# Layer-norm roots moved to GpSimd, min before exp replaced by Relu and exp on ScalarE, in a one-core transformer block

## The chip, the core and the metric

The kernel runs on one NeuronCore of a Trainium2 chip. The core has five engines with instruction streams of their own: TensorE (PE) for matrix products and transposes, VectorE (DVE), ScalarE (ACT), GpSimd (POOL) and SyncE (SP, which here only issues DMAs). They meet through semaphores. The metric is the device time of one execution in microseconds. One launch computes everything, in fp32.

## The reference

16 images of 3x96x96 pixels pass through one block of a vision transformer of width 192, with 38 tokens per image, so 608 tokens.

```python
h = patches @ W_emb + b_emb                  # 36 patches of 768 values, two class tokens in front
h = h + pos_embedding
xh = (h - mean(h)) / sqrt(var(h) + 1e-5)     # first layer norm
q, k, v = split(xh @ qkv_w.T)                # 12 heads of 16
f = lambda x: elu(x) + 1                     # feature map of queries and keys
# three linear attentions on f(q), f(k), v: a window of 12, every third key, 12 anchors;
# blended with softmax weights, then out_w
h = h + blended @ out_w.T
x2 = (h - mean(h)) / sqrt(var(h) + 1e-5)     # second layer norm
# 8 experts 192 -> 768 -> 192 with Relu, each token goes to its best 2,
# weighted by the two renormalised softmax probabilities
h = h + mixture(x2)
```

The feature map is elu(x) + 1 = max(x, 0) + exp(min(x, 0)).

## The kernel before

The tokens are cut into six groups: five of three images (114 tokens) and a last one of one image (38 tokens). A group lies with one token per partition, so the statistics of a layer norm are one column per group.

**Stages.** First the image patches are transposed and embedded (to about 26 us of the profiled execution). Then comes the attention as a software pipeline written out by hand, a loop over `t` on each of PE, DVE and ACT. In step `t` they project group `t`, take the key sums of group `t-1`, spread the queries of `t-2`, multiply keys and values of `t-3`, form the heads and the residual of `t-4` and start the router of `t-5` (to about 162 us). Each row is then scattered twice by indirect DMA to the region of its expert in HBM. At last a loop runs over 17 tiles of 128 slots (PE lines 940 to 976), and their results are added to the output sums by indirect DMA.

**What sets the order.** There is no planner. Each engine runs its instructions in the order of its block in the source, and a `wait_ge` holds all that stands behind it on that engine.

**A layer norm of a group.** DVE's `moments` (lines 1051 to 1054) writes mean and variance to `mv`. ACT's `root` (lines 1383 to 1387) takes the square root of the variance plus `epsv` into `rstd`. DVE's `normalise` (lines 1056 to 1061) waits for it, inverts it (line 1059) and makes the normalised tile (line 1060): `xhat` for the first layer, `tokens_out` for the second. PE transposes the tile of the first layer (`xhat_turn`, line 654), ACT copies it out (`xhat_out`), and PE projects queries and keys (line 677) and values (line 681). Only after the first of these does PE embed groups 2 and 3.

**The feature map.** In `features` (lines 1082 to 1097) DVE takes the minimum with zero of the 384 columns of queries and keys from PSUM into `qkmin`. ACT's line 1514 makes the exponential `qkexp`. DVE then combines them with the maximum into `qtok` and `ktok` (lines 1095, 1096).

**Function tables.** ACT's exponential and its square root are in different tables, and before an activation whose table is not loaded the program has an ACT_TABLE_LOAD. Copies and Relus are used with either.

**POOL.** After some small constants it waits for the bias of the experts (`b1_in`, line 1597) and splits it into a high and a low part (lines 1598, 1599). Then, group by group, it masks the values (line 1626, tile `vm`), spreads them over the heads (line 1635, tile `vexp`), copies normalised rows (`copy_row`) and issues the scatters (`scatter`, line 1612). The helper `link` puts a wait for an instruction's own completion behind each.

## Time and profile before

| | |
|---|---|
| median of 3 runs | 267.15 us |
| the runs | 267.15, 264.56, 270.74 us |
| profiled execution | 268.69 us, its span 266.9 us |
| mean granted PE clock | 0.855 of full speed |
| PE busy | 223.2 us (84%) |
| PE weight loads busy | 191.6 us (72%) |
| DVE busy | 150.5 us (56%), 464 instructions |
| ACT busy | 110.5 us (41%), 252 instructions |
| POOL busy | 73.7 us (28%), 103 instructions |

The span runs from the first to the last instruction of the profiled execution; what lies around it is 268.69 - 266.9 = 1.8 us. Busy time says how much an engine does, not whether somebody waits for it; for that the chain of waits is read, which is followed back from the last instruction. ScalarE's table loads count as busy. In the windows, "clock" is the TensorE clock that was granted, 1.00 being 2.4 GHz and 0.50 being 1.2 GHz.

### The profile page before, as it was taken

The page shows a single profiled execution, that of the slowest core. Times are in us where ns is not written, and L with a number is a line of the kernel's source. Part 1 is how long each engine was busy: PE and PEld are TensorE (multiplying, and loading weights), DVE is VectorE, ACT ScalarE, POOL GpSimd, SP SyncE. Part 2 cuts the span into 40 slices and gives each one's busy share as a digit, 9 for nine tenths or more (in the row PEclk, how much of TensorE's full clock was granted, in tenths as well). Part 3 has the DMA queues.
Part 4 walks back from the last instruction along what each step waited for, and adds up shares of the span by engine and source line. Part 5 has one row for each costly group of instructions (what it writes and reads, how often), then busy time and mean ns, then how long its engine had stood idle before and what let it go on. Part 6 is the DMA issues. An engine that isn't in the chain of part 4 may idle for free.

```text
span 266.9 us, 4475 instructions
## 1 busy us (share of the span) xinstructions
PE 223.2 (84%) x1340; PEld 191.6 (72%) x1340; DVE 150.5 (56%) x464; ACT 110.5 (41%) x252; POOL 73.7 (28%) x103
## 2 busy tenths in 40 slices
PE   6379699796999999998989955189999999999950
PEld 6268399564697967876767752079999999999940
DVE  5234318859476957858575688756768443433300
ACT  2343463767133453726242478035433342424210
POOL 4001260073305050414221335001324242423330
PEclk9658659799799999999985555559999999999995
DMA  7999999999400000000101298351333334341213
GB/s 121 132 233 172 235 287 271 266 225 289 123 10 0 0 4 1 2 0 0 29 2 26 56 324 205 80 136 42 70 47 59 47 54 52 52 55 18 29 15 85
DMA packets 26259, 25.73 MB, mean 96 GB/s; under 512 B 4970, under 2 KB 23261, under 8 KB 26221
## 3 DMA queue, kind: packets, MB, share of 16 engines
q1 hardware_dynamic: 22333, 22.16, 35.1%
q0 software_dynamic: 3568, 2.64, 7.8%
q10 hardware_dynamic: 336, 0.66, 1.7%
q8 instruction: 12, 0.20, 0.3%
q14 instruction: 10, 0.08, 0.1%
HBM read 16.56 MB, written 7.77 MB: 91 GB/s over the span
## 4 chain that ended last, share of the span: by engine, by line
PE 62%; DVE 14%; DMA 11%; issue 4%; ACT 3%; POOL 2%; SPq 2%; DVEq 0%; POOLq 0%; ACTq 0%
PE ps L950 11%; PE ps L973 10%; PE ps L580 5%; PE ps L708 4%; DMA wemb<-in_L_tok_W_emb 4%; DMA sums<-ys,xs 4%; PE ps L798 4%; PE ps L712 4%; PE ps L784 4%; PE ps L677 3%; PE ps L962 3%; PE ps L691 2%; DMA sent<-row,index 2%; SPq L428 1%; POOL sent L1612 1%
## 5 line engine op out<-in xcount | busy, mean ns | idle before, releaser
L1648 POOL DMA_INDIRECT sums<-ys,xs x17 | 26.3, 1546 | 67.0 <-ACT ys L1548 60.7
L973 PE MATMUL ps<-w2s,hidT 128*128 x204 | 36.1, 327 | 1.1 <-DVE hidT L1352 0.8
L973 PEld LDWEIGHTS ps<-w2s,hidT 128*128 128x128 f32 x204 | 33.2, 189 | 2.0 <-issue 1.6
L950 PE MATMUL ps<-w1hi,xhi 128*128 x68 | 25.3, 372 | 1.4 <-DVE xhi L1332 0.8
L1548 ACT ACTIVATE ys<-ps,xs 128x192 f32<-128x192 f32 x17 | 7.2, 421 | 40.0 <-PE ps L973 37.6
L1331 DVE TENSOR_TENSOR xlo<-ps,xhi 128x128 fp32r<-128x128 f32 x17 | 5.0, 292 | 29.8 <-ACT xend L1541 29.8
L784 PE MATMUL ps<-vm,ktok 114*96 114x288 f32 (+1 forms) x48 | 15.6, 406 | 5.0 <-DVE kvb L1147 5.0
L1635 POOL COPY vexp<-vtok 114x32 f32<-114x32 f32 (+1 forms) x36 | 8.0, 222 | 41.4 <-PE ps L712 39.5
L1430 ACT ACTIVATE qlb<-ps,cst 96x228 f32<-96x228 f32 (+1 forms) x36 | 12.1, 425 | 17.2 <-PE ps L746 17.2
L1612 POOL DMA_INDIRECT sent<-row,index x12 | 13.5, 1128 | 18.1 <-DVE row L1219 14.8
L708 PE MATMUL ps<-at,vexp 114*96 114x114 f32 (+1 forms) x144 | 18.2, 281 | 0.0
L798 PE MATMUL ps<-qlb,kT 96*114 96x342 f32 (+1 forms) x48 | 17.3, 442 | 0.5 <-DVE h L1068 0.5
L580 PE MATMUL ps<-wemb,xT 128*114 128x192 f32 (+1 forms) x72 | 17.3, 400 | 0.4 <-DMA wemb<-in_L_tok_W_emb 0.4
L708 PEld LDWEIGHTS ps<-at,vexp 114*96 114x96 f32 (+1 forms) x144 | 16.4, 181 | 1.2 <-issue 0.8
L1147 DVE TENSOR_TENSOR kvb<-ps,cst 96x288 f32<-96x288 f32 (+1 forms) x24 | 10.0, 418 | 11.5 <-PE ps L784 11.4
L1626 POOL TENSOR_TENSOR vm<-vtok,cst 114x576 f32<-114x576 f32 (+1 forms) x12 | 13.8, 1147 | 7.4 <-PE ps L784 5.8
L580 PEld LDWEIGHTS ps<-wemb,xT 128*114 128x114 f32 (+1 forms) x72 | 14.1, 214 | 1.9 <-DMA wemb<-in_L_tok_W_emb 0.7
L712 PE MATMUL ps<-qx,kvb 96*96 96x114 f32 (+1 forms) x128 | 15.3, 268 | 0.0
L950 PEld LDWEIGHTS ps<-w1hi,xhi 128*128 128x128 f32 x68 | 13.4, 196 | 2.4 <-issue 2.4
L962 PE MATMUL ps<-cst,hid 128*128 128x128 f32 x102 | 14.2, 276 | 0.0
L712 PEld LDWEIGHTS ps<-qx,kvb 96*96 96x96 f32 x128 | 13.8, 169 | 0.3 <-issue 0.3
L1346 DVE TENSOR_SCALAR hid<-ps 128x384 f32<-128x384 f32 x17 | 9.4, 554 | 7.6 <-PE ps L950 7.6
(197 smaller groups left out, 486.3 us busy)
## 6 DMA issues: line engine op xcount, KB each, us to landing
w2s<-in_L_ffn_W SPq DMA_DIRECT2D x8, 576.0 KB, 8.0
sent<-blank SPq DMA_DIRECT2D x1, 3977.0 KB, 32.3
w1s<-in_L_ffn_W SPq DMA_DIRECT2D x4, 768.0 KB, 17.1
xs<-sent SPq DMA_DIRECT2D x17, 96.0 KB, 1.9
w1s<-in_L_ffn_W SPq DMA_DIRECT2D x4, 384.0 KB, 18.5
w1hi<-w1hi SPq DMA_DIRECT2D x8, 192.0 KB, 3.9
ximg<-in_x SPq DMA_DIRECT2D x12, 96.0 KB, 9.3
w1s<-in_L_ffn_b SPq DMA_DIRECT2D x1, 792.0 KB
```

The source lines that it names most:

```text
L580: ins = pe.matmul(ps[6 + g % 2][0:n, 0:D], xT[:, k, t0:t0 + n], wemb[:, k, :], start=(k == 0), stop=(k == KCH - 1))
L708: pe.matmul(o, vexp[0:n, g % 2, i * HH + hh, :], at[0:n, g % 2, i * HH + hh, 0:w], start=(hh == 0), stop=False, skip_group_check=True)
L712: last = pe.matmul(o, kvb[:, g % 2, i, kind * PER + b, :], qx[:, g % 2, kind, i, b * GTOK:b * GTOK + w], start=False, stop=(kind == 1 and ...
L784: pe.matmul(ps[5][0:HALF, 0:imgs * HALF], ktok[0:n, g % KS, i * HALF:(i + 1) * HALF], vm[0:n, g % 2, i, kind * PER:kind * PER + imgs, :], ...
L798: pe.matmul(ps[6][0:n, 0:3 * n], kT[:, g % 3, i, 0:n], qlb[:, g % 2, i, 3 * (m % 2):3 * (m % 2) + 3, 0:n], start=True, stop=True).then_inc ...
L950: last = pe.matmul(ps[2 + c][:, 0:PASS], xx, of_expert(ww, expert), start=(n == 0), stop=(n == len(products) - 1))
L962: last = pe.transpose(ps[4 + c][:, k * 128:(k + 1) * 128], hid[:, (3 * c + k) * 128:(3 * c + k + 1) * 128], ident)
L973: last = pe.matmul(ps[6 + j % 2][:, 0:D], hidT[:, k, :], of_expert(w2s[:, :, k, :], expert), start=(k == 0), stop=(k == FCH - 1))
L1430: ins = ac.activation(qlb[:, g % 2, :, hh, 0:n], turned_q, ACT.Copy, scale=blk[:, hh * HD:hh * HD + 1])
L1612: po.indirect_dma_start(sent.rearrange("r p c -> (r p) c"), bass.IndirectOffsetOnAxis(ap=index[0:n, g, k:k + 1], axis=0), row[0:n, g, k, : ...
L1626: link(po.tensor_tensor(vm[0:n, g % 2, i], v.unsqueeze(1).broadcast_to([n, 2 * PER, HALF]), vmask[0:n, :].unsqueeze(2).broadcast_to([n, 2 ...
L1648: po.indirect_dma_start(sums, bass.IndirectOffsetOnAxis(ap=xs[:, j % NS, D + TAIL + 1:].bitcast(U32), axis=0), ys[:, j % 2, :], None, comp ...
```

## The change

The root and its inversion become one power: POOL adds the epsilon to the variance and raises the sum to -0.5, with two instructions on one column, each behind a semaphore wait. DVE's inversion goes. The minimum moves from DVE to ACT, as Relu of -x, and the exponential is taken of the negated result. With no square root left, ACT needs one table. POOL's programme is written out anew: the roots of groups 0 and 1 come right behind the bias split, those of groups 2 to 5 before the spread of the values, and those of the second layer after the `head_values` of two groups later; `copy_row` and `scatter` move around them.

```diff
--- before.py
+++ after.py
@@ -166,7 +166,7 @@
         stats = sb("stats", [GTOK, GROUPS, 6])
         mv = sb("mv", [GTOK, GROUPS, 2])
         rstd = sb("rstd", [GTOK, GROUPS])
-        epsv = sb("epsv", [GTOK, 1])
+        mhalf = sb("mhalf", [GTOK, 1])
         ones = sb("ones", [GTOK, 128])
         lead = sb("lead", [1, 1])
         row = sb("row", [GTOK, GROUPS, TOP, ROW])
@@ -335,7 +335,7 @@
 
         dv = sem("dv")
         dv_qx_zero = sem("dv_qx_zero")
-        dv_eps = sem("dv_eps")
+        dv_mhalf = sem("dv_mhalf")
         dv_posb_zero = sem("dv_posb_zero")
         dv_class_zero = sem("dv_class_zero")
         dv_one = sem("dv_one")
@@ -346,7 +346,6 @@
         dv_embedded = sem("dv_embedded")
         dv_moments = sem("dv_moments")
         dv_xhat = sem("dv_xhat")
-        dv_min = sem("dv_min")
         dv_features = sem("dv_features")
         dv_key_sums = sem("dv_key_sums")
         dv_image_sums = sem("dv_image_sums")
@@ -375,7 +374,7 @@
         ac_band_exp = sem("ac_band_exp")
         ac_anchor_exp = sem("ac_anchor_exp")
         ac_base = sem("ac_base")
-        ac_root = sem("ac_root")
+        ac_min = sem("ac_min")
         ac_weights = sem("ac_weights")
         ac_anchor_sum = sem("ac_anchor_sum")
         ac_xhat_turned = sem("ac_xhat_turned")
@@ -407,6 +406,7 @@
         gp_masked_values = sem("gp_masked_values")
         gp_head_values = sem("gp_head_values")
         gp_row = sem("gp_row")
+        gp_root = sem("gp_root")
 
         block = ctx.enter_context(nc.Block())
 
@@ -1019,7 +1019,7 @@
             ve.memset(ones[:], 1.0).then_inc(dv_one, 1)
             ve.memset(posb[0:1, :], 0.0).then_inc(dv_posb_zero, 1)
             ve.memset(xT[:].rearrange("p k (b s) -> p k b s", s=SEQ)[:, :, :, 0:2], 0.0).then_inc(dv_class_zero, 1)
-            ve.memset(epsv[:], EPS_LN).then_inc(dv_eps, 1)
+            ve.memset(mhalf[:], -0.5).then_inc(dv_mhalf, 1)
             ve.memset(qx[:], 0.0).then_inc(dv_qx_zero, 1)
             ve.wait_ge(dv_class_zero, 1)
 
@@ -1055,8 +1055,7 @@
 
             def normalise(g, n, src, dst, layer):
 
-                ve.wait_ge(ac_root, GROUPS * layer + g + 1)
-                link(ve.reciprocal(rstd[0:n, g:g + 1], rstd[0:n, g:g + 1]))
+                ve.wait_ge(gp_root, 2 * (GROUPS * layer + g + 1))
                 return ve.tensor_scalar(dst, src, mv[0:n, g, 0:1], rstd[0:n, g:g + 1],
                                         ALU.subtract, ALU.mult)
 
@@ -1083,10 +1082,6 @@
 
                 t0, n, _ = group(g)
                 src = ps[2][0:n, 0:2 * D]
-                ve.wait_ge(pe_qk, g + 1)
-                if g >= 1:
-                    ve.wait_ge(ac_exp, g)
-                ve.tensor_scalar(qkmin[0:n, :], src, 0.0, None, ALU.min).then_inc(dv_min, 1)
                 ve.wait_ge(ac_exp, g + 1)
                 if g >= 2:
                     ve.wait_ge(dv_queries, g - 1)
@@ -1378,13 +1373,6 @@
             ac.activation(anc[2][:], anc[1][:], ACT.Exp).then_inc(ac_anchor_exp, 1)
             ac.wait_ge(pe_base, 1)
             ac.activation(hbase[:], ps[5][0:GTOK, 0:D], ACT.Copy).then_inc(ac_base, 1)
-            ac.wait_ge(dv_eps, 1)
-
-            def root(g, layer):
-
-                t0, n, _ = group(g)
-                ac.wait_ge(dv_moments, GROUPS * layer + g + 1)
-                ac.activation(rstd[0:n, g:g + 1], mv[0:n, g, 1:2], ACT.Sqrt, bias=epsv[0:n, :]).then_inc(ac_root, 1)
 
             def xhat_out(g):
 
@@ -1394,8 +1382,6 @@
                               xhat_bank(g)[0:HALF, 0:2 * GTOK].rearrange("p (i t) -> p i t", i=2)[:, :, 0:n],
                               ACT.Copy).then_inc(ac_xhat_turned, 1)
 
-            root(0, 0)
-            root(1, 0)
             for m in range(4):
                 i, r3 = m // 2, m % 2
                 ac.wait_ge(pe_weights_turned, m + 1)
@@ -1491,7 +1477,6 @@
                     attention_over(ac)
                     ac.wait_ge(w1_in, 16 * E)
                     weights_high(0)
-                    root(GROUPS - 1, 1)
                     x2_out(GROUPS - 1)
                     weight(GROUPS - 2)
                     combine_out(0)
@@ -1508,10 +1493,12 @@
                     weight(t - 6)
                 if t < GROUPS:
                     t0, n, _ = group(t)
-                    ac.wait_ge(dv_min, t + 1)
+                    ac.wait_ge(pe_qk, t + 1)
+                    ac.activation(qkmin[0:n, :], ps[2][0:n, 0:2 * D], ACT.Relu, scale=-1.0).then_inc(ac_min, 1)
+                    ac.wait_ge(ac_min, t + 1)
                     if t >= 1:
                         ac.wait_ge(dv_features, t)
-                    ac.activation(qkexp[0:n, :], qkmin[0:n, :], ACT.Exp).then_inc(ac_exp, 1)
+                    ac.activation(qkexp[0:n, :], qkmin[0:n, :], ACT.Exp, scale=-1.0).then_inc(ac_exp, 1)
                     ac.wait_ge(pe_v, t + 1)
                     if t >= 3:
                         ac.wait_ge(gp_head_values, HH * (t - 2))
@@ -1519,12 +1506,7 @@
                 if t == 0:
                     anchors_out()
                     xhat_out(1)
-                    root(2, 0)
                     turning_over(ac)
-                if t + 3 < GROUPS:
-                    root(t + 3, 0)
-                if 0 <= t - 4 < GROUPS - 1:
-                    root(t - 4, 1)
                 if t >= GROUPS + 3:
                     weights_high(t - GROUPS - 2)
             weight(GROUPS - 1)
@@ -1613,11 +1595,16 @@
                                           bass.IndirectOffsetOnAxis(ap=index[0:n, g, k:k + 1], axis=0),
                                           row[0:n, g, k, :], None).then_inc(sent_in, 16)
 
-            patches_over(po)
-            for g in range(GROUPS):
+            def root(g, layer):
+
+                n = group(g)[1]
+                po.wait_ge(dv_moments, GROUPS * layer + g + 1)
+                link(po.tensor_scalar(rstd[0:n, g:g + 1], mv[0:n, g, 1:2], EPS_LN, None, ALU.add), gp_root)
+                link(po.tensor_tensor(rstd[0:n, g:g + 1], rstd[0:n, g:g + 1], mhalf[0:n, :], ALU.pow), gp_root)
+
+            def masked_values(g):
+
                 t0, n, imgs = group(g)
-                if g >= 4:
-                    copy_row(g - 4)
                 po.wait_ge(ac_v, g + 1)
                 if g >= 2:
                     po.wait_ge(pe_keys_values, 4 * (g - 1))
@@ -1625,21 +1612,50 @@
                     v = vtok[0:n, g % 3, i * HALF:(i + 1) * HALF]
                     link(po.tensor_tensor(vm[0:n, g % 2, i], v.unsqueeze(1).broadcast_to([n, 2 * PER, HALF]),
                                           vmask[0:n, :].unsqueeze(2).broadcast_to([n, 2 * PER, HALF]), ALU.mult), gp_masked_values)
-                if g == 0:
-                    turning_over(po)
-                    embedding_over(po)
-                    link(po.memset(vexp[:], 0.0), gp_vexp_zero)
+
+            def head_values(g):
+
+                n = group(g)[1]
                 if g >= 2:
                     po.wait_ge(pe_heads, g - 1)
                 for hh in range(HH):
                     link(po.tensor_copy(
                         vexp[0:n, g % 2].rearrange("p (i a) c -> p i a c", i=2)[:, :, hh, hh * HD:(hh + 1) * HD],
                         vtok[0:n, g % 3].rearrange("p (i c) -> p i c", i=2)[:, :, hh * HD:(hh + 1) * HD]), gp_head_values)
+
+            po.wait_ge(dv_mhalf, 1)
+            root(0, 0)
+            root(1, 0)
+            patches_over(po)
+            masked_values(0)
+            root(2, 0)
+            root(3, 0)
+            masked_values(1)
+            root(4, 0)
+            root(5, 0)
+            turning_over(po)
+            embedding_over(po)
+            link(po.memset(vexp[:], 0.0), gp_vexp_zero)
+            head_values(0)
+            head_values(1)
+            for g in range(2, GROUPS):
+                masked_values(g)
+                head_values(g)
+                root(g - 2, 1)
+                if g >= 3:
+                    copy_row(g - 3)
             po.wait_ge(sent_blank, 16)
-            for g in range(GROUPS - 4, GROUPS + 2):
-                if g < GROUPS:
-                    copy_row(g)
-                scatter(g - 2)
+            scatter(0)
+            copy_row(3)
+            scatter(1)
+            root(4, 1)
+            copy_row(4)
+            scatter(2)
+            root(5, 1)
+            copy_row(5)
+            scatter(3)
+            scatter(4)
+            scatter(5)
             po.wait_ge(sums_in, 16 * (GROUPS + 1))
             for j in range(TILES):
                 po.wait_ge(ac_answers, j + 1)
```

## Rows read from the trace of the kernel before

**Rows 1.** The chain that ended last, 27 to 47 us: start, us, what.

```profile
27.19 1.28 ACT L1387
...
28.49 0.48 ACT rstd L1387 x2
...
30.60 2.87 PE ps L677 x4
...
46.63 0.47 DVE qkmin L1089
```

**Rows 2.** Timeline of DVE: start, us, line, operation, what ended the idle time.

```profile
26.93 0.18 DVE L1054 BATCH_NORM_AGGREGATE mv<-stats 114x2 f32<-114x6 f32 x1
...
28.81 0.16 DVE L1059 RECIPROCAL rstd<-rstd 114x1 f32<-114x1 f32 x1 [0.85 <-ACT rstd L1387]
29.01 0.38 DVE L1060 TENSOR_SCALAR xn<-h,mv,rstd 114x192 f32<-114x192 f32 x1
```

**Rows 3.** Timeline of POOL, 27 to 36 us, columns as in rows 2.

```profile
27.30 0.19 POOL L1593 CAST blank<-cst 128x1 uint32<-128x1 f32 x1
...
32.73 0.81 POOL L1598 CAST b1hi<-b1s 8x768 fp32r<-8x768 f32 x1 [4.64 <-DMA w1s<-in_L_ffn_b]
33.62 1.80 POOL L1599 TENSOR_TENSOR b1lo<-b1s,b1hi 8x768 fp32r<-8x768 f32 x1
```

**Rows 4.** Timeline of PE.

```profile
29.45 0.61 PE L654 MATMUL ps<-cst,xn 114*96 114x114 f32 x2 [2.02 <-DVE xn L1060]
...
44.95 1.46 PE L677 MATMUL ps<-wT,xhT 96*114 96x384 f32 x4
...
129.47 0.41 PE L784 MATMUL ps<-vm,ktok 38*96 38x96 f32 x2
```

**Rows 5.** Windows: length, busy us (instructions) of PE, PEld, DVE, ACT, POOL; clock; DMA.

```profile
27.00:30.00 3.00, 0.97 (x8) 0.45 (x5) 1.89 (x8) 2.80 (x7) 0.85 (x5) 0.87 1.02 196
...
30.00:33.00 3.00, 2.46 (x5) 1.40 (x5) 0.00 (x0) 0.45 (x2) 0.27 (x1) 0.50 1.05 290
...
38.00:40.00 2.00, 2.00 (x9) 1.98 (x8) 0.00 (x0) 0.62 (x1) 0.84 (x1) 0.63 0.99 321
...
200.00:262.00 62.00, 57.08 (x369) 55.74 (x367) 23.86 (x51) 20.57 (x59) 21.48 (x14) 0.99 0.31 42
```

**Rows 6.** Groups of ACT by shape: count, busy us, mean ns, idle before.

```profile
L1387 ACT ACT_TABLE_LOAD x10 | 12.8, 1283 | 1.2 <-DVE mv L1054 1.1
...
L1514 ACT ACT_TABLE_LOAD x5 | 6.4, 1283 | 3.9 <-DVE qkmin L1089 3.8
...
L1445 ACT ACT_TABLE_LOAD x5 | 6.4, 1283 | 0.1
...
L1558 ACT ACTIVATE hid<-ps 128x384 f32<-128x384 f32 x17 | 8.4, 491 | 10.6 <-PE ps L950 10.6
...
L1514 ACT ACTIVATE qkexp<-qkmin 114x384 f32<-114x384 f32 x5 | 2.6, 523 | 11.7 <-DVE qkmin L1089 11.7
```

**Rows 7.** Group of DVE, columns as in rows 6.

```profile
L1089 DVE TENSOR_SCALAR qkmin<-ps 114x384 f32<-114x384 f32 (+1 forms) x6 | 3.3, 554 | 8.8 <-PE ps L677 8.8
```

**Rows 8.** The chain that ended last, 143 to 155 us.

```profile
143.56 0.19 DVE mv L1054
...
143.78 0.30 ACT rstd L1387
...
144.31 0.38 DVE row L1060
...
153.53 0.18 DVE mv L1054
```

**Rows 9.** Timeline of POOL, 112 to 152 us.

```profile
112.21 2.36 POOL L1626 TENSOR_TENSOR vm<-vtok,cst 38x576 f32<-38x576 f32 x2 [0.34 <-PE ps L784]
...
150.94 1.11 POOL L1612 DMA_INDIRECT sent<-row,index  x1 [0.30 <-issue]
```

**Rows 10.** Timeline of DVE, second layer norm of the third group.

```profile
114.89 0.18 DVE L1054 BATCH_NORM_AGGREGATE mv<-stats 114x2 f32<-114x6 f32 x1
```

## The prediction

> **What bounds the kernel now.** I read the 40 slices of the page first. TensorE (PE) is nearly full from the middle of the attention on, and in the last third, the mixture of experts, it is busy for 57.1 of 62 us at the granted clock 0.99 [rows 5]. The change touches nothing there, so it can only move the start of that stage. Then the chain of waits over the first 60 us. Up to 30.6 us it runs through the embedding, the moments of group 0, a table load, the root and the turned weights into the first projection of queries and keys [rows 1]. From there it is PE or VectorE (DVE) work that follows the projection of each group in a fixed order. The question is therefore when the first normalised tile is ready, and after that which removed or added piece stands on the chain.
>
> **The early stretch: the first root.** The moments of group 0 are ready at 26.93 + 0.18 = 27.11 us [rows 2]. ScalarE (ACT) then loads a table for 1.28 us and takes roots 0 and 1 from 28.49 [rows 1]. DVE inverts (28.81) and normalises from 29.01 [rows 2], and PE, which has nothing else it may do, turns that tile at 29.45 after 2.02 us of waiting [rows 4].
>
> The change puts this root on GpSimd (POOL), whose instructions run in the order written. Ahead of it stand the bias split (lines 1597 to 1599) and its wait for the bias DMA; the diff leaves both where they are. POOL waits 4.64 us for that DMA, makes the high part at 32.73, and the low part from 33.62 for 1.80 us, so it is free at 35.42 [rows 3]. The moments are done 8.3 us earlier and no longer decide. A root now costs two POOL instructions on one column, each followed by a wait on its own semaphore. A cast of one column takes 0.19 us on POOL, and the step over such a wait is 33.62 - (32.73 + 0.81) = 0.08 [rows 3]. I take the 0.19 for the addition. The power is in no row: it can cost what the cast does, 0.19, or, as software that computes more per element, up to the 1.80 us of the longest two-operand instruction here [rows 3]. I take 0.4, near the lower end, because it is one element per partition like the cast, where the 1.80 is for 768.
>
> So the first normalisation starts at 35.42 + 0.08 + 0.19 + 0.08 + 0.40 + 0.04 = 36.21 instead of 29.01: **+7.2 us** (0.04 is the step to another engine, 143.78 - 143.74 in [rows 8]). Behind the waiting POOL instruction queue the masks of the values, which need values that are themselves late by the same amount. Behind DVE's wait for the root stands the whole DVE programme, behind PE's wait the first projection. Nobody has independent work to fill the gap: PE stands idle from 27.43 to about 36.6. The table load of 1.28 us and the inversion leave this place, but they were finished long before POOL gets there, so they give nothing back here. No other early wait ends on something fixed in time, so I see nothing that absorbs the shift.
>
> **The other roots.** Before, from the end of the moments to the start of the normalisation took 144.31 - 143.74 = 0.57 us with the table already loaded [rows 8]. Now it is 0.04 + 0.19 + 0.08 + 0.40 + 0.04 = 0.75 us, 0.18 more. DVE waits for it at three places: group 2 in the first layer and the last two groups in the second (153.53 is the other one [rows 8]). Together **+0.5 us**. The bounds of the power make it -0.1 to +4.7.
>
> The other eight roots have slack, though POOL now waits for moments before it masks further values. The tightest is the third group of the second layer: its moments end at 115.07 [rows 10], so the masks of the last group, which started at 112.21 and took 2.4 us [rows 9], start at about 116 relative to this stretch; PE wants them at 129.47 [rows 4]. The root of the last group stands behind two scatters, of which the second ends at 152.05, before its moments at 153.70; for the group before it the same order has more slack [rows 8, 9]. Their cost is 0 with 1.6 us of cover; if that cover is gone, the excess counts in full.
>
> **The minimum and the exponential.** DVE loses 6 instructions of 0.55 us [rows 7] and ACT gains 6. The nearest row for the new Relu is the one on a 384-column PSUM tile, 491 ns, against 523 for the exponential from SBUF [rows 6]. The pair still follows the projection. On the chain it stands twice, for groups 1 and 2. For group 1 PE was done at 46.41 [rows 4] and DVE, busy with the query scaling, began the minimum at 46.56, on the chain from 46.63 [rows 1]; ACT is free and can begin 0.1 us sooner. For each of the two the piece itself is 0.55 against 0.49 [rows 6, 7]. For the later groups PE has other work and the pair is hidden. Together **-0.2 us**.
>
> **Inversions and table loads.** Twelve inversions of 0.16 us leave DVE [rows 2]. Those on the chain that the sums above do not hold are of groups 3, 4 and 5 in the first layer: **-0.5 us**. The 20 table loads, 10 + 5 + 5 of 1283 ns, free 25.7 us of ACT [rows 6]. ACT is not what is waited for: only one of the loads, at 27.19, is on the chain, and it is the one overtaken by the bias split. All others were issued while their operand was not there yet or beside PE work. They count 0, down to -1 us if one of them hid a wait that the trace gives to another engine. The single 59 ns memset is exchanged for another.
>
> **Sum.** 7.2 + 0.5 - 0.2 - 0.5 = **+7.0 us**. Against the profiled execution (span 266.9, time 268.69) that is 273.9 and 275.7. The median of the runs shown is 267.15, 1.5 below that execution, so I predict 267.15 + 7.0 = 274.15, in round numbers **274 us**. A measurement of this kernel tells about 2%, 5.3 us, from no change (its own runs spread from 264.56 to 270.74).
>
> **Rivals.**
> *A slow power.* If the power, or its first call, takes the 1.80 us of the far row, it counts at four places: 4 x 1.4 = 5.6 more, 279.8 us. Against: the first cast took 0.19 without a first-call cost [rows 3]. The Trainium skill (GPSIMD Engine Reference, section 2.1, Instruction dispatch) says that the first call to a freshly loaded GpSimd routine pays roughly 6 us; by that the sum would be 280, and the casts and multiplications here show no such pause. Chance 0.11.
>
> *Not slower, through PE's clock.* The granted clock falls from 1.0 to 0.50, its 1.2 GHz level, between 27 and 30 us and comes back at about 39.5 [rows 5], so some 9 us of work after the first wait run at half speed. If the clock returned at the same moment although work starts at 37.6, 7 us of that work would take 3.5 us: +3.5 net, 270.7 us. It decides from 1.7 us given back, and a bias DMA that lands 2 us sooner would bring it to 268.7. Against: the clock fell during idleness and came back only after work, and here there is more idleness. Chance 0.15.
>
> *Faster, because ACT was a hidden bound.* If the 25.7 us of loads had stood between PE's pieces in a way the chain misattributes, half of them would outweigh the shift: 267.15 + 7.0 - 12.9 = 261.3. The trace speaks against it: the load at 27.19 ends at 28.47 and the root starts at 28.49 [rows 1], and the exponentials sat idle for 11.7 us behind the minimum [rows 6]. The Trainium skill (ScalarE: Activation LUTs, section "What ACT_TABLE_LOAD costs") adds a drain of about 1380 ns to each 1283 ns load, 53 us in all; the 0.02 us behind this load do not show it, and the trace decides. Chance 0.04.
>
> **Chances and range.** My forecast has 0.70, and within it about one in six that less than 5.3 us is left (a bias DMA that lands 1 to 2 us sooner against the moments, a cheap power, spread of the medians). Slower by over 2%: 0.59 + 0.11 = 0.70. Within 2%: 0.11 + 0.15 = 0.26. Faster: 0.04. The forecast alone spans 271 to 277. To hold 8 in 10 the range reaches down to the middle of the clock case, 270, and up to most of the slow power, 279.
>
> **What would show it.** After the change POOL's first root starts right behind the low part of the bias, at about 35.5 us. PE then shows about 9 us of idle time before line 654, ended by DVE's normalisation. No table load follows the first. The first projection starts near 37.7. The stage from the first expert tile on keeps its length, and the Relu takes about 0.5 us. A root of more than 1 us on POOL proves the first rival; a first projection at 31 us, or a POOL that reaches the root before 30, proves my main term wrong; a clock back up within 4 us of the first projection proves the second.

## The result and the profile after

The kernel after takes 277.02 us (median of 4 runs, 275.24 to 278.46), the kernel before took 268.27 beside it (4 runs, 264.56 to 270.74). The ratio is 1.042, with a 95% interval of 1.028 to 1.056: slower. In all of its 55 runs here the kernel before falls in two groups, 16 runs at 262.0 to 264.8 us (the lower, median 263.8) and 39 at 266.9 to 271.7 (the upper), and the ratio, which leaves out runs more than 1.5% above a kernel's fastest, compares 276.9 with 265.9 (the mean of 264.56 and 267.15), a rise of 11.1 us. Forecast was 274, by +7.0. The direction and the range held, the size did not: the rise is 8.75 us by the medians, 11.1 by the ratio, and 13.2 against the lower group. The profiled execution took 275.24 us, its span is 273.1.

Head of the page: instructions, busy time of each engine with its share of the span, and the clock in 40 slices.

```profile
span 273.1 us, 4461 instructions
PE 218.8 (80%) x1340; PEld 187.2 (69%) x1340; DVE 148.0 (54%) x446; ACT 84.8 (31%) x226; POOL 83.6 (31%) x127
...
PEclk9999559979799999999995555559999999999995
```

ACT is busy for 25.7 us less than the 110.5 of before, as the 20 table loads of [rows 6] are gone, and the kernel is slower all the same. POOL is busy for 9.9 us more.

The chain that ended last, 18 to 40 us (start, us, what). It answers to [rows 1].

```profile
18.43 13.69 DMA w1s<-in_L_ffn_b
...
33.15 1.80 POOL b1lo L1581
...
35.36 0.58 POOL rstd L1603
...
37.56 2.88 PE ps L677 x4
```

Nothing of the embedding or the moments stands on it any more. It goes back from the first projection through the root to the low part of the bias and to the DMA that brings the bias, which lands at 18.43 + 13.69 = 32.12 us. POOL's timeline (start, us, operation, and in brackets the idle time before it with its releaser) answers to [rows 3].

```profile
32.25 0.81 POOL L1580 CAST b1hi<-b1s 8x768 fp32r<-8x768 f32 x1 [6.13 <-DMA w1s<-in_L_ffn_b]
33.14 1.79 POOL L1581 TENSOR_TENSOR b1lo<-b1s,b1hi 8x768 fp32r<-8x768 f32 x1
35.03 0.25 POOL L1602 TENSOR_SCALAR rstd<-mv 114x1 f32<-114x1 f32 x1
35.36 0.57 POOL L1603 TENSOR_TENSOR rstd<-rstd,mhalf 114x1 f32<-114x1 f32 x1
...
52.47 2.38 POOL L1613 TENSOR_TENSOR vm<-vtok,cst 114x576 f32<-114x576 f32 x2 [3.31 <-ACT vtok L1505]
...
64.96 2.02 POOL L1638 MEMSET vexp<- 114x2304 f32 x1
```

The first root starts 0.1 us behind the low part, as forecast. The power takes 0.57 us, without a longer first call. DVE's timeline answers to [rows 2, 8]: the moments of group 0, the first-layer normalisations of groups 0, 3 and 5, and one normalisation of the second layer.

```profile
24.93 0.18 DVE L1054 BATCH_NORM_AGGREGATE mv<-stats 114x2 f32<-114x6 f32 x1
...
35.97 0.39 DVE L1059 TENSOR_SCALAR xn<-h,mv,rstd 114x192 f32<-114x192 f32 x1 [10.00 <-POOL rstd L1603]
...
53.68 1.28 DVE L1059 TENSOR_SCALAR xn<-h,mv,rstd 114x192 f32<-114x192 f32 x1
...
65.65 1.43 DVE L1059 TENSOR_SCALAR xn<-h,mv,rstd 38x192 f32<-38x192 f32 x1
...
148.52 0.18 DVE L1054 BATCH_NORM_AGGREGATE mv<-stats 114x2 f32<-114x6 f32 x1
...
149.72 0.38 DVE L1059 TENSOR_SCALAR row<-h,mv,rstd 114x192 f32<-114x192 f32 x1 [0.89 <-POOL rstd L1603]
```

Three things are to be seen. DVE waits 10.00 us for the first root. The same normalisation, 0.34 to 0.39 us long elsewhere, takes 1.28 and 1.43 us while POOL is in the masks (52.47 to 54.85) and in the memset (64.96 to 66.98); each ends 0.1 us after POOL's instruction. And from the end of the moments to the normalisation it is now 149.72 - 148.70 = 1.02 us, where it was 0.57.

Groups by shape (count, busy us, mean ns, idle before):

```profile
L1603 POOL TENSOR_TENSOR rstd<-rstd,mhalf 114x1 f32<-114x1 f32 x10 | 5.7, 570 | 0.8
...
L1602 POOL TENSOR_SCALAR rstd<-mv 114x1 f32<-114x1 f32 x10 | 2.4, 241 | 20.0 <-DVE mv L1054 19.7
...
L1497 ACT ACTIVATE qkmin<-ps 114x384 f32<-114x384 f32 x5 | 2.5, 491 | 17.4 <-PE ps L677 17.4
...
L1362 ACT ACT_TABLE_LOAD x1 | 1.3, 1283 | 4.0 <-issue 4.0
```

Windows (length, busy us and instructions of PE, PEld, DVE, ACT, POOL; clock; DMA), to be read against [rows 5]:

```profile
28.00:32.00 4.00, 0.00 (x0) 0.00 (x0) 0.00 (x0) 0.00 (x0) 0.00 (x0) 0.50 1.05 275
36.00:40.00 4.00, 3.05 (x6) 1.64 (x7) 0.73 (x2) 0.36 (x1) 0.80 (x2) 0.50 1.04 279
40.00:44.00 4.00, 4.00 (x26) 3.64 (x25) 0.71 (x2) 2.58 (x7) 1.67 (x2) 0.79 1.05 281
```

The last three columns are the granted clock, the DMA share and GB/s. The clock is at its 1.2 GHz level when work resumes and back about 4 us after the first projection begins; before, it took 9 us [rows 5].

Stage by stage, in the two profiled executions and in a second one of the kernel before (b2_before_again, below), in us from the start of the span:

| | before | before again | after |
|---|---|---|---|
| moments of group 0 end | 27.11 | 24.94 | 25.11 |
| first normalisation starts | 29.01 | 26.84 | 35.97 |
| projection of group 0 (line 677) | 30.60 | 28.37 | 37.56 |
| of group 1 | 44.95 | 43.33 | 49.57 |
| of group 2 | 54.37 | 52.92 | 59.63 |
| last moments, second layer | 153.70 | 151.95 | 159.41 |
| first product of the experts | 175.13 | 173.50 | 181.14 |
| last sum of outputs | 259.19 | 257.69 | 265.26 |

All of the rise arises before the first normalisation: +6.96 in the first pair, +9.13 against the second. From group 0 to group 1 some 2 to 3 us come back, in the stretch where the clock is back sooner, and 0.5 to 0.6 are lost again up to group 2. The stage of the experts is unchanged (84.06, 84.19, 84.12).

### The profile page after: what moved, and what is told of

It reads as the page before. It is cut to its first block, busy times and chain, and to the rows that moved or that the text cites. A ratio compares the mean times of both kernels' runs of the same rounds, so it can differ in the third digit from the quotient of the medians.

```text
span 273.1 us, 4461 instructions
## 1 busy us (share of the span) xinstructions
PE 218.8 (80%) x1340; PEld 187.2 (69%) x1340; DVE 148.0 (54%) x446; ACT 84.8 (31%) x226; POOL 83.6 (31%) x127
## 4 chain that ended last, share of the span: by engine, by line
PE 58%; DMA 16%; DVE 12%; issue 4%; POOL 4%; SPq 2%; ACT 2%; POOLq 0%; DVEq 0%; ACTq 0%
PE ps L950 11%; PE ps L973 10%; DMA w1s<-in_L_ffn_b 5%; PE ps L708 4%; DMA ximg<-in_x 4%; DMA sums<-ys,xs 4%; PE ps L798 4%; PE ps L677 4%; PE ps L712 4%; PE ps L784 4%; PE ps L580 3%; PE ps L962 3%; PE ps L691 2%; SPq L428 2%; DMA sent<-row,index 2%
## 5 line engine op out<-in xcount | busy, mean ns | idle before, releaser
L1613 POOL TENSOR_TENSOR vm<-vtok,cst 114x576 f32<-114x576 f32 (+1 forms) x12 | 13.8, 1150 | 11.9 <-ACT vtok L1505 8.7
L580 PE MATMUL ps<-wemb,xT 128*114 128x192 f32 (+1 forms) x72 | 14.8, 359 | 0.0
L580 PEld LDWEIGHTS ps<-wemb,xT 128*114 128x114 f32 (+1 forms) x72 | 11.8, 183 | 1.6 <-issue 0.3
```

What stands on the lines that cost most here:

```text
L580: ins = pe.matmul(ps[6 + g % 2][0:n, 0:D], xT[:, k, t0:t0 + n], wemb[:, k, :], start=(k == 0), stop=(k == KCH - 1))
L1613: link(po.tensor_tensor(vm[0:n, g % 2, i], v.unsqueeze(1).broadcast_to([n, 2 * PER, HALF]), vmask[0:n, :].unsqueeze(2).broadcast_to([n, 2 ...
```

## The experiments

In the edits, `split` stands for the three lines of the bias: the wait for it and the two instructions that split it. Shifts are between medians of all runs where nothing else is said.

**e1_roots_first: the bias split behind the first two roots.**

```diff
-            split
             po.wait_ge(dv_mhalf, 1)
             root(0, 0)
             root(1, 0)
+            split
```

> The changed kernel with the roots of groups 0 and 1 moved ahead of the bias split on POOL; all else as changed. Theory (the bias wait is the cost): the first root starts with the moments, at 25 to 27 us instead of 35, the first normalisation by 28, and the time falls by 7 to 9 us to 268 to 270; the moments still carry the later costs. Rival (the clock takes most of it back in any case): the time falls by under 5 us, because in the changed kernel PE ran the work after the gap at the higher clock sooner. Rival (the POOL instructions themselves, twelve roots of 0.9 us, are the cost): the time stays within 2 us of the changed kernel.

Measured: 266.76 us (265.10 to 268.20, 10 runs), ratio to before 1.013 (1.007 to 1.018). POOL's timeline, and the first normalisation on DVE:

```profile
26.57 0.25 POOL L1599 TENSOR_SCALAR rstd<-mv 114x1 f32<-114x1 f32 x1
26.90 0.58 POOL L1600 TENSOR_TENSOR rstd<-rstd,mhalf 114x1 f32<-114x1 f32 x1
...
31.55 0.81 POOL L1627 CAST b1hi<-b1s 8x768 fp32r<-8x768 f32 x1 [3.11 <-DMA w1s<-in_L_ffn_b]
```

```profile
27.51 0.39 DVE L1059 TENSOR_SCALAR xn<-h,mv,rstd 114x192 f32<-114x192 f32 x1 [1.19 <-POOL rstd L1600]
```

Three lines moved take 277.02 - 266.76 = 10.3 us away, more than the 7 to 9 expected. Between the two profiled executions (275.24 and 266.71) it is 8.5, and that is the shift of the first normalisation, 35.97 - 27.51 = 8.46, carried through to the end. The place of the root in POOL's queue is the main cause. By the ratio e1 is still 1.3% slower than the kernel before.

**e2_gate_alone: the kernel before, with the same wait and nothing else of the change.**

```diff
             embedded(1)
+            ve.wait_ge(gp_bias_split, 2)
             xhat(0)
```

> The kernel before, with one wait added: DVE waits for the bias split before it normalises group 0. No root, no minimum and no table is changed. Theory (the bias wait is the cost): the first normalisation moves from 29.0 to about 35.5 us and the time rises by 5 to 9 us over the kernel before, 273 to 277. Rival (roots on POOL and lost overlap are the cost): it rises by under 3 us.

Measured: 274.12 us (270.64 to 278.66, 10 runs), ratio 1.028 (1.016 to 1.040).

```profile
35.56 0.38 DVE L1060 TENSOR_SCALAR xn<-h,mv,rstd 114x192 f32<-114x192 f32 x1
```

The gate alone makes the kernel slower. Its price depends on what it is held against. The 25 runs of the kernel before beside it have a median of 269.85, mostly from the upper group, and against that it is 4.3 us, less than the 5 to 9 expected. Against the lower group (seven of the 25, median 263.71) the six runs of e2 from 270.64 to 274.45, median 273.3, are 9.6 us longer, near what the gate gives back in e1. The traces agree with both: against b2_before_again, an execution of the upper group, the first normalisation is 35.56 - 26.84 = 8.7 us later, and the projection of group 1 only 49.20 - 43.33 = 5.9, because b2_before_again has the low clock for 10 us after its first projection. Against e9_before_warm (below), where the clock stays up, it is 7.7 at the projection of group 0 and 49.20 - 39.42 = 9.8 at that of group 1. The profiled execution of e2 is its longest (278.66) and loses more in the second layer.

**e4_pool_order: the masks of group 1 and the fill of `vexp` moved among the roots.**

```diff
             masked_values(0)
             root(2, 0)
             root(3, 0)
-            masked_values(1)
             root(4, 0)
-            root(5, 0)
+            masked_values(1)
             turning_over(po)
             embedding_over(po)
             link(po.memset(vexp[:], 0.0), gp_vexp_zero)
+            root(5, 0)
             head_values(0)
```

> The changed kernel with its POOL order altered in the first layer: root 4 before the masks of group 1, and root 5 behind the clearing of the spread values instead of before it. The bias split stays first. Theory of a second cost (two normalisations on DVE stand still until the POOL instruction beside them ends, 1.28 and 1.43 us instead of 0.38): both come down to about 0.4 and the time falls by 1 to 2 us, to 275 to 276. Rival (those two stalls are hidden, or not caused by POOL): the two normalisations keep their length, or the time does not move by more than 0.5 us.

Measured: 271.79 us (10 runs: six from 270.3 to 272.0, four from 278.2 to 280.1), 5.2 below after, where 1 to 2 were expected. DVE and POOL:

```profile
54.03 0.35 DVE L1059 TENSOR_SCALAR xn<-h,mv,rstd 114x192 f32<-114x192 f32 x1
...
63.74 0.36 DVE L1059 TENSOR_SCALAR xn<-h,mv,rstd 38x192 f32<-38x192 f32 x1
```

```profile
55.46 2.38 POOL L1613 TENSOR_TENSOR vm<-vtok,cst 114x576 f32<-114x576 f32 x2
...
57.91 2.02 POOL L1637 MEMSET vexp<- 114x2304 f32 x1
```

The two long normalisations are short again once POOL's instruction no longer lies beside them. That is 0.93 + 1.07 = 2.0 us. In the profiled execution another 1.4 us come from the bias, which lands sooner (the first normalisation starts at 34.60 instead of 35.97), and have nothing to do with the edit; the rest is in the next experiment.

**e5_first_and_order: the edits of e1 and e4 together.**

> The changed kernel with both edits: roots 0 and 1 ahead of the bias split, and the POOL order in which neither the masks of group 1 nor the clearing of the spread values lies beside a normalisation. If both costs are real and add, the time is 3 to 5 us under the 266.8 of the kernel with the first edit alone: 262 to 264. If the second cost was only there because the gap had shifted the stages, it stays within 1 us of 266.8.

Measured: 263.05 us (eight runs from 261.43 to 264.02, two of 269.95 and 271.31), against 267.87, ratio 0.995 (0.988 to 1.001), so no worse than before and perhaps a little better. Against e1 the order is worth 3.7 us, and against e4 the place of the first root 8.7 (8.1 between the profiled executions, where the first normalisation is 34.60 - 26.61 = 8.0 us earlier). How 2 us of stall become more is seen on PE. In the kernel after it waits for the stalled normalisation, and what follows runs slow:

```profile
55.02 0.40 PE L654 MATMUL ps<-cst,xn 114*96 114x114 f32 x2 [0.97 <-DVE xn L1059]
...
56.48 3.22 PE L580 MATMUL ps<-wemb,xT 128*38 128x192 f32 x12
```

In e5 it does not wait, and the same 12 products of the embedding take a third less:

```profile
44.18 0.40 PE L654 MATMUL ps<-cst,xn 114*96 114x114 f32 x2
...
45.36 2.14 PE L580 MATMUL ps<-wemb,xT 128*38 128x192 f32 x12
```

The windows show the clock; first after, then e5:

```profile
54.00:58.00 4.00, 3.03 (x14) 2.04 (x14) 3.35 (x8) 2.50 (x8) 1.79 (x3) 0.66 0.93 224
```

```profile
46.00:49.00 3.00, 3.00 (x15) 1.76 (x13) 2.58 (x6) 1.64 (x6) 2.85 (x3) 1.00 1.11 293
```

From the projection of group 1 to that of group 2 it is 10.06 us in after and 10.13 in e1, and 7.83 and 7.82 in e4 and e5. e3b_warm_40 (below) parts the two terms: it has the order of the kernel after and the stall of 1.28 us, but the clock at 1.00, and takes 53.85 - 45.10 = 8.75. So of the 2.2 us the stall is 0.9 and the low clock 1.3. That the stall brings the low clock about is not shown: the kernel before (9.42) and e6 (9.77) have the low clock at this place without a stall there.

**e6_first_min_dve: e5 with the minimum back on DVE.**

```diff
+                ve.tensor_scalar(qkmin[0:n, :], src, 0.0, None, ALU.min).then_inc(dv_min, 1)
...
-                    ac.activation(qkmin[0:n, :], ps[2][0:n, 0:2 * D], ACT.Relu, scale=-1.0).then_inc(ac_min, 1)
-                    ac.activation(qkexp[0:n, :], qkmin[0:n, :], ACT.Exp, scale=-1.0).then_inc(ac_exp, 1)
+                    ac.activation(qkexp[0:n, :], qkmin[0:n, :], ACT.Exp).then_inc(ac_exp, 1)
```

> The same kernel as the one with both edits, but with the minimum back on DVE and a plain exponential on ACT; roots stay on POOL and no table is loaded twice. My price for the move of the minimum was 0.2 us gained on the chain: within 0.5 us of the kernel with both edits. Rival (Relu and exponential in a row on ACT shorten the path of each group): 1 to 2 us slower than it.

Measured: 266.72 us (263.93 to 270.88, 10 runs), 3.7 above e5, where at most 0.5 was expected, ratio to before 1.007 (1.000 to 1.013). The piece itself is 0.06 us longer. But in its profiled execution the clock is down at the place where e5 keeps it, and group 1 to group 2 takes 9.77 us:

```profile
46.00:50.00 4.00, 4.00 (x17) 2.18 (x16) 3.62 (x6) 2.70 (x9) 2.52 (x3) 0.62 1.10 302
```

**e10_relu_alone: the kernel before with only the minimum as a Relu on ACT** (the roots stay on ACT, with their table loads).

```diff
-                ve.tensor_scalar(qkmin[0:n, :], src, 0.0, None, ALU.min).then_inc(dv_min, 1)
...
+                    ac.activation(qkmin[0:n, :], ps[2][0:n, 0:2 * D], ACT.Relu, scale=-1.0).then_inc(ac_min, 1)
```

> The kernel before with only the minimum moved: Relu and exponential on ACT, roots and inversions where they were, 20 table loads kept. My price for this part is 0.2 us gained. If instead this part carries the gain that the kernel with both edits shows over the kernel before (268 to 263), it is 3 us or more under the kernel before. If the table loads stand in the way of the Relu on ACT, it is 1 to 3 us over it.

Measured: 268.37 us (267.45 to 268.94, 4 runs) against 268.94. By the medians the move alone gives -0.6 here, near the forecast of -0.2. But all four runs lie in the upper group, 4.5 us above the two lower ones of the seven beside it (263.00 and 264.71). With 39 of 55 runs of the kernel before in the upper group, four in a row come by chance about one time in four, so this does not show whether the move keeps the kernel out of the lower group. What the minimum on DVE costs in e6, the low clock or something else, stays open.

**e3_warm_gap and e3b_warm_40: the kernel after, with matrix products that nobody reads in PE's gap,** 80 and 40 of them.

```diff
             turn_projections()
+            for n in range(80):
+                pe.matmul(ps[0][:, 0:128], ones[:], ones[:], start=True, stop=True)
             xhat_turn(0)
```

> The changed kernel with 80 matmuls of 128 columns, whose result nobody reads, on PE between the weight transposes and the first normalised tile, so that PE is not idle while the bias is waited for. They take about 8.6 us of the 11 us gap. If the clock after the gap costs anything, the first projection takes 1.3 us instead of 2.9 and the whole stretch up to the third embedding is 2 to 4 us shorter: 273 to 275 against 277. If the clock rival explains nothing, the time stays within 1 us.

> The changed kernel with 40 unread matmuls in the gap instead of 80: in the run with 80 they took 18.1 us, twice what I had reckoned, and pushed the first projection from 37.6 to 44.05. 40 take 9.0 us and fit in the gap. Clock rival: the first projection stays at 37 to 38 and takes 1.5 us instead of 2.9, and the time falls by 2 to 4 us against the changed kernel, 273 to 275. Otherwise it stays within 1 us of it.

Measured: 80 products give 282.51 us (279.69 to 284.13, 4 runs), ratio 1.049 (1.042 to 1.057). I had them too short. They take 18 us and end long after the root:

```profile
25.26 18.06 PE L660 MATMUL ps<-ones 114*128 114x128 f32 x160
...
44.05 1.52 PE L679 MATMUL ps<-wT,xhT 96*114 96x384 f32 x4 [0.54 <-ACT xhT L1383]
```

That run says nothing on its question, except that the projection takes 1.52 us at full clock instead of 2.88. The 40 products end in time (projection at 35.10, clock 1.00 from 26 to 62 us): 273.71 us (269.33 to 279.59, 4 runs), 3.3 below after. Four runs that spread over 10 us do not size it, and the profiled one owes 2.25 us to a bias that lands sooner (first normalisation at 33.72). The stages do: from the projection of group 0 to that of group 2 it takes 18.75 us, and in the kernel after 22.07, so the clock held is worth 3.3. It is not a part of the gate's price, as e1, which has no gate, needs 22.35 for the same stretch.

**b2_before_again: the kernel before, a second profile.**

> The kernel before, unchanged, for a second trace: its 25 runs lie in two groups, 262.0 to 264.8 and 267.3 to 271.7. If the groups differ by TensorE's clock, a trace of the lower group shows no stretch at the 1.2 GHz level during the embedding or between 46 and 56 us, and its moments of group 0 end near 25 us instead of 27.1. If they differ by DMA, the images or the embedding weights land at another time.

Measured: 267.14 us, so an execution of the upper group again; no trace shows the lower one. The moments end at 24.94, and the clock was full from about 18 us on, where in the first profile it was low up to 22. So a slow embedding is not what makes the upper group. The clock is low for 10 us after the first projection:

```profile
28.37 2.88 PE L677 MATMUL ps<-wT,xhT 96*114 96x384 f32 x4 [0.69 <-ACT xhT L1393]
```

```profile
32.00:36.00 4.00, 4.00 (x19) 3.87 (x18) 0.72 (x2) 3.92 (x8) 3.74 (x3) 0.50 1.05 278
36.00:40.00 4.00, 4.00 (x18) 3.97 (x18) 1.05 (x4) 0.69 (x2) 1.18 (x2) 0.69 1.03 247
```

**e9_before_warm: the kernel before with 8 such products; e8_best_warm: e5 with 8.** Both have the loop of e3 ahead of `xhat_turn(0)`:

```diff
+            for n in range(8):
+                pe.matmul(ps[0][:, 0:128], ones[:], ones[:], start=True, stop=True)
             xhat_turn(0)
```

> The kernel before with the same 8 unread matmuls before the first normalised tile. If the upper of its two groups of runs (267 to 272) is the one in which the clock stays low for 9 to 10 us after the first projection, nearly all runs move to the lower group, 261 to 265. If the groups come from elsewhere, they stay as they are, about a third low and two thirds high.

> The kernel with both edits and 8 unread matmuls (1.8 us) on PE between the weight transposes and the first normalised tile. If TensorE's clock falls because of that short idle stretch, it stays at 1.00 through the first projection, the stretch from first to second projection shrinks from 11.7 to about 10 us, and the time is 260 to 262. If it falls in any case, the time stays within 1 us of 263.

Measured: e9 262.93 us (262.60, 262.62, 263.23, 268.12), 6.0 below the 268.94 beside it and 0.9 below the lower group; e8 262.41 us (261.66 to 268.19, 5 runs), as e5. In e9 the gap is closed and the clock stays up, until 44 us:

```profile
28.33 0.40 PE L654 MATMUL ps<-cst,xn 114*96 114x114 f32 x2 [0.21 <-DVE xn L1062]
29.43 1.52 PE L679 MATMUL ps<-wT,xhT 96*114 96x384 f32 x4 [0.69 <-ACT xhT L1395]
```

```profile
32.00:36.00 4.00, 4.00 (x29) 4.00 (x29) 1.62 (x5) 3.97 (x8) 3.78 (x3) 1.00 1.04 267
```

Three of e9's four runs lie at the level of the lower group, of the kernel before 16 of 55; by chance three or more of four come about one time in thirteen. That the two groups of the kernel before are a matter of the clock behind this gap is likely from this and the traces, but not shown. Against it as the whole account: the mean granted clock does not order the runs (0.880 in those near 267.2, 0.867 in those near 264), and e10's profiled execution has the clock back at 32 us and took 267.45.

e8 missed its forecast, and the trace says why. The first projection takes 1.52 us instead of e5's 2.57, but the projection of group 1 does not come sooner: 39.82 against 39.67. What was won is waited away for the root of group 2, which stands on POOL behind the bias split and the masks of group 0, though its moments are ready at 34.27:

```profile
33.82 2.38 POOL L1612 TENSOR_TENSOR vm<-vtok,cst 114x576 f32<-114x576 f32 x2
...
36.60 0.57 POOL L1602 TENSOR_TENSOR rstd<-rstd,mhalf 114x1 f32<-114x1 f32 x1
```

```profile
37.20 0.38 DVE L1061 TENSOR_SCALAR xn<-h,mv,rstd 114x192 f32<-114x192 f32 x1 [2.93 <-POOL rstd L1602]
```

So the gate on the bias is only moved in e5 and e8, from the root of group 0 to that of group 2. As to the worth of the change with its queueing mended: e5, e8 and e9 all lie at 262.4 to 263.1, and against a kernel before with its clock held there is nothing left that can be measured. They have the lowest medians of all.

**e7_power_thrice: e5 with each root's power made three times** (the two extra results go to a spare column).

```diff
+                link(po.tensor_tensor(lead2[0:n, :], rstd[0:n, g:g + 1], mhalf[0:n, :], ALU.pow))
+                link(po.tensor_tensor(lead2[0:n, :], rstd[0:n, g:g + 1], mhalf[0:n, :], ALU.pow))
                 link(po.tensor_tensor(rstd[0:n, g:g + 1], rstd[0:n, g:g + 1], mhalf[0:n, :], ALU.pow), gp_root)
```

> The kernel with both edits, each root with two more powers of the same column into a spare column ahead of the one that counts, 1.3 us more per root (0.57 and a step of 0.07 each). My working had DVE wait for a root at four places: 4 x 1.3 = 5.2 us more, 268 to 269 against 263.05. If the roots are hidden, it stays within 1 us; if also the roots that I called covered are waited for (group 3 of the first layer, or those that masks queue behind), it rises by 7 us or more.

Measured: 274.94 us (270.34 to 277.38, 4 runs), 11.9 above e5, where 5.2 was expected. The waits that ended DVE's idle time (total us, count, longest), first e7, then e5:

```profile
DVE xn L1060 <- POOL rstd L1603: 7.0, 4, 2.4
...
DVE row L1060 <- POOL rstd L1603: 4.4, 2, 2.2
```

```profile
DVE xn L1059 <- POOL rstd L1600: 2.8, 3, 1.2
...
DVE row L1059 <- POOL rstd L1600: 1.9, 2, 1.0
```

The waits grow by 11.4 - 4.7 = 6.7 us. The roots' cost is therefore on the path, at more places than I counted. The other 5 us are not attributed by rows. The granted clock is lower (0.833 against 0.876) in the profiled execution, which with 277.20 us is 15.0 above e5's; 6.5 of that are there by the projection of group 1, as the clock is low up to 40 us, and in e5 only to 32.

## Why the prediction was right in direction and short in size

**What bounds the kernel:** right. The experts' stage kept its length, and the whole effect is in when the early stages start.

**The step that failed is the size of "The first root: +7.2".** Its mechanism is right. Forecast were a start of the root right behind the low part, a normalisation at 36.21 and no more table loads; measured 35.97, and +6.96 against the profile before. But taken away (e1), the same gate moved the first normalisation by 8.46 and the time by 8.5 (profiled executions) to 10.3 us (medians), and 8.0, 8.1 and 8.7 with the other order (e4 to e5). The start of 29.01 that I subtracted comes from an execution whose embedding ran at the low clock, as this row of the kernel before shows:

```profile
20.00:22.00 2.00, 2.00 (x11) 1.99 (x10) 0.66 (x1) 0.81 (x2) 0.00 (x0) 0.50 1.12 210
```

The other traces of kernels that leave the embedding alone have the moments ready at 24.4 to 26.1 us instead of 27.11, while POOL starts on the bias at 30.0 to 32.7 whatever the rest does. A gate fixed in time costs more the earlier its waiter is ready: 35.97 - 26.84 = 9.1 against b2_before_again. The start of the sum was off as well: 267.15, the median of three runs, lies in the upper group, whose two traced executions take 2.3 and 3.0 us longer from the first projection to the second than the kernel after does.

**"Their cost is 0" failed as well.** I looked for masks that come too late and found cover, and that cover held: the last group's masks start at 121.89, PE wants them at 134.64. What I did not price is that the moved order lays POOL's long instructions beside DVE's normalisations. One such stall stood in the trace of before, where I could have read it:

```profile
58.78 0.79 DVE L1060 TENSOR_SCALAR xn<-h,mv,rstd 114x192 f32<-114x192 f32 x1
```

The order costs 3.7 us (e1 to e5; 5.2 from after to e4), of which 2.0 are the stalls; 1.3 us more is PE work at the low clock between the projections of groups 1 and 2, whose tie to the stall is not shown. The Trainium skill (GPSIMD Engine Reference, section 1, Specifications) says that GpSimd's SBUF interfaces are shared with VectorE, with contention for some of VectorE's forms; the 1.28 and 1.43 us against 0.35 agree with that, but no run here changed the form of the instruction.

**The other roots:** +0.5 forecast. The power is 0.57 and the addition 0.24 us, where I had 0.40 and 0.19, and the path from moments to normalisation grew by 0.45 instead of 0.18: 3 x 0.45 = 1.35, 0.85 more, within the bounds given. A slow power did not appear, at the first call neither (0.57 us). In one place I had read too little: the root of group 2 also stands behind the bias split, and becomes the bound once the first is out of the way (e8).

**The minimum and the exponential:** -0.2 forecast; -0.6 measured by medians in e10, and 3.7 from e6 to e5. The two disagree, and the price is not settled. The Relu takes the 491 ns of [rows 6]. **Inversions at -0.5:** no run separates them. **Table loads at 0:** nothing speaks against it; e9, which keeps all 20, is as fast as e5, which has none of them.

**The clock rival was true in part.** Its sign came: in the profile after the clock is back about 4 us after the first projection begins, 5 us sooner than before, which gives 2.3 us between groups 0 and 1 (14.35 to 12.01), less than the 3.5 of the rival. I had the two as exclusive cases; they are one kernel. Nor is it the longer gap that brings the clock back sooner: e1 and e5 have no gap of that kind and need 12.22 and 11.68 us for the same stretch.

**The balance, by medians.** From e5 to the kernel after it is 3.7 (order) and 10.3 (bias ahead of the root), or in the other sequence 8.7 and 5.2 (by way of e4): 14.0 either way, which is no more than the difference of 277.02 and 263.05. e5 itself is 0.7 below the lower group of the kernel before (263.8), and that, taken from 14.0, leaves the rise of 13.2 against that group. Against the median of 268.27 only 8.75 of it show, because that median is of the upper group. e5 lies at the lower level in 8 of 10 runs, the kernel before in 16 of 55. The forecast did not have the second loss and started from an upper value, and that 277.02 lies only 3 us above 274 is in part luck.

**Open.** What decides whether the clock is back 4 or 10 us after the first projection: gaps of about 2 us stand in executions of both kinds. Why three of the four runs of the kernel after are 1.1 to 3.2 us above the profiled one, and why e4's runs fall in two groups, no trace shows. Neither does one show the lower group of the kernel before. That POOL's instruction beside them makes the stalls is shown by e4 and e5, where both vanish; that it does so through shared access to SBUF is inferred.

## What to carry to other kernels

Before an operation is moved to an engine that runs in order, find what that engine waits for ahead of the new place: here three lines moved were worth 8.5 to 10 us, more than anything that the operation itself costs. Then look for the next operation behind the same wait: in e8 it was the root of group 2. Price such a gate from more than one execution, because its end is fixed by a DMA while the start of the wait moves with the clock, and ask to which of a kernel's groups of runs the execution belongs: the gate of e2 is 4.3 us against one median and 9.6 against the other. And ask of a freed resource who waited for it: 25.7 us of table loads were removed from ACT, and e9, which keeps them, is as fast as e5.

## What the runs showed of the hardware

- A power of one column by one column on GpSimd, 114 partitions in fp32, takes 570 ns, an addition 241 ns, and the first power no longer than the others (0.57 us).
- A DVE normalisation of 192 columns took 1.28 and 1.43 us instead of 0.35 beside a GpSimd multiplication and a GpSimd memset, and ended 0.1 us after them.
- With eight products that nobody reads in a 2 us gap of PE, three of four runs of the kernel before took 262.6 to 263.2 us, the median 6.0 below the one beside it: the projection behind the gap took 1.52 instead of 2.88 us, and the granted clock stayed at 1.00 up to 44 us.
- In e5 the same products shortened that projection from 2.57 to 1.52 us and the time by nothing, as DVE then waited 2.93 instead of 1.07 us for a root on GpSimd.
- One kernel's runs fall in two groups (262.0 to 264.8 and 266.9 to 271.7), with nothing between 264.8 and 266.9.
